# Offsets split earlier, constants on GpSimd, and three smaller moves in a fused GroupNorm, gating and deformable-convolution kernel

## The reference, cut to what matters

```python
def _L0(pair, Wa, ba, Wb, bb, Wg, bg, Wo, bo):     # gated products of the rows
    a = pair @ Wa + ba
    b = pair @ Wb + bb
    g = sigmoid(pair @ Wg + bg)
    ab = einsum('bijk,bikl->bijl', a, b)
    return g * ab @ Wo + bo

def _L1(x, w_off, b_off, w_def):                   # deformable 3x3 convolution
    x = relu(x)
    offset = conv3x3(x, w_off) + b_off             # 18 channels: dy, dx for 9 taps
    py, px = base_y + offset[:, :, 0], base_x + offset[:, :, 1]
    samp = bilinear_gather(x, py, px)              # 9 samples per pixel
    return einsum('bckhw,ock->bohw', samp, w_def)

x = x + _L0(group_norm(x), ...)
x = x + _L1(group_norm(x), ...)
```

## Time and profile before

| what | value |
|---|---|
| runs | 1631.22, 1642.09, 1646.17 us |
| profiled execution | 1645.54 us, span 1643.7 us, 28193 instructions |
| PE busy | 1543.9 us, 94% of the span |
| DVE busy | 1111.5 us, 68% |
| ACT busy | 1052.1 us, 64% |
| POOL busy | 934.0 us, 57% |
| granted clock of PE, mean | 0.986 of full speed |
| DMA | 356.56 MB, mean 217 GB/s |
| chain that ended last | PE 61%, issue 12%, POOL 8%, DVE 8%, DMA 6%, ACT 2% |

### The profile page before, as it was taken

How to read it: one execution, slowest core, us unless ns; L and a number is a source line. 1 busy time by engine, 2 the same in 40 slices (tenths; PEclk the granted TensorE clock), 3 DMA queues, 4 the chain that set the end, 5 groups by cost and what they waited for, 6 DMA issues and landing times.

```text
span 1643.7 us, 28193 instructions
## 1 busy us (share of the span) xinstructions
PE 1543.9 (94%) x9875; PEld 1129.6 (69%) x9876; DVE 1111.5 (68%) x1910; ACT 1052.1 (64%) x1500; POOL 934.0 (57%) x734
## 2 busy tenths in 40 slices
PE   4999999937999999999999999999999999999997
PEld 3777787715776667776666676766777677767775
DVE  5988888745666666666666666666666666666653
ACT  2555555527676767767667666666777777666662
POOL 2555555716755555655665656566566566656562
PEclk9999999958999999999999999999999999999999
DMA  4343344246767777777776777777767777777672
GB/s 138 107 119 106 118 118 118 75 166 241 262 260 247 253 240 268 252 253 246 247 251 243 242 252 255 246 249 272 261 237 256 254 256 268 261 243 247 242 238 67
DMA packets 145701, 356.56 MB, mean 217 GB/s; under 512 B 10709, under 2 KB 77808, under 8 KB 145584
## 3 DMA queue, kind: packets, MB, share of 16 engines
q1 hardware_dynamic: 130864, 327.90, 59.1%
q10 hardware_dynamic: 14720, 27.14, 4.7%
HBM read 292.14 MB, written 62.85 MB: 216 GB/s over the span
## 4 chain that ended last, share of the span: by engine, by line
PE 61%; issue 12%; POOL 8%; DVE 8%; DMA 6%; ACT 2%; SPq 0%; ACTq 0%; POOLq 0%; DVEq 0%
PE bank L759 24%; PE pair L731 17%; PE pair L805 7%; DMA hx_all<-hat_x 6%; POOL samples_hi L1496 4%; PE bank L777 4%; DVE offs_lo L1276 3%; PE pair L777 3%; POOL weights L1541 2%; DVE offs_hi L1273 2%; PE pair L742 2%; PE pair L744 2%; ACT samples_hi L985 1%; POOL rstd L1470 1%; POOL samples_lo L1483 1%
## 5 line engine op out<-in xcount | busy, mean ns | idle before, releaser
L1541 POOL TENSOR_TENSOR weights<-hy_all,hx_all 126x512 f32<-126x512 f32 x576 | 756.6, 1343 | 522.0 <-DMA hx_all<-hat_x 381.6
L1300 DVE SCALAR_TENSOR_TENSOR samples_lo<-bank,samples_hi 128x432 f16<-128x432 f32 (+1 forms) x704 | 403.4, 591 | 364.7 <-ACT samples_hi L985 351.5
L759 PE MATMUL bank<-weights,zT 126*128 126x216 f32 (+1 forms) x2816 | 583.0, 344 | 2.7 <-POOL weights L1541 2.3
L759 PEld LDWEIGHTS bank<-weights,zT 126*128 126x128 f32 x2816 | 490.2, 190 | 44.0 <-issue 29.2
L985 ACT ACTIVATE samples_hi<-bank 128x432 f16<-128x432 f32 (+1 forms) x704 | 362.4, 519 | 226.3 <-PE bank L759 216.2
L731 PE MATMUL pair<-samples_hi,w_hi 128*128 128x512 f16 x576 | 218.9, 380 | 1.2 <-DVE y L1334 1.2
L731 PE MATMUL pair<-samples_lo,w_hi 128*128 128x512 f16 x576 | 217.7, 378 | 0.0
L731 PE MATMUL pair<-samples_hi,w_lo 128*128 128x512 f16 x576 | 217.6, 378 | 0.0
L994 ACT COPY zT<-pair 126x512 f32<-126x512 f32 x192 | 112.5, 586 | 112.2 <-PE pair L777 108.0
L927 ACT ACTIVATE z<-raw,norm_band 128x2772 f32<-128x2772 f32 (+3 forms) x80 | 180.0, 2270 | 0.0
L1483 POOL TENSOR_TENSOR samples_lo<-samples_hi,samples_lo 128x512 f16<-128x512 f32 x64 | 74.2, 1159 | 131.1 <-ACT samples_lo L888 131.0
(11 more groups left out here) (138 smaller groups left out, 1944.8 us busy)
## 6 DMA issues: line engine op xcount, KB each, us to landing
hy_all<-hat_y SPq DMA_DIRECT2D x192, 648.0 KB
hx_all<-hat_x SPq DMA_DIRECT2D x192, 648.0 KB
raw<-x_pad SPq DMA_DIRECT2D x68, 272.0 KB, 11.2
x_pad<-hy_all SPq DMA_DIRECT2D x64, 272.0 KB, 3.3
weights<-in_x SPq DMA_DIRECT2D x64, 256.0 KB, 2.9
out<-y SPq DMA_DIRECT2D x32, 512.0 KB, 10.6
hat_y<-hats ACTq DMA_DIRECT2D x64, 252.0 KB
hat_x<-hats ACTq DMA_DIRECT2D x64, 162.0 KB
```

Source lines behind the costliest of these rows:

```text
L759: mm = nc.tensor.matmul(sampled_pair(b)[:, :, at:at + BR * cols], zT[0:WPIX, w, :], weights[0:WPIX, u, :, w * WC * BR:(w * WC + cols) * BR ...
L1300: nc.vector.scalar_tensor_tensor(out=samples_lo[:, u, :, c0:c1], in0=sampled_pair(b)[:, :, 0:c1 - c0], scalar=1.0, in1=samples_hi[:, u, :, ...
L1541: nc.gpsimd.tensor_tensor(weights[0:WPIX, u, k, :], hy_all[0:WPIX, k, :], hx_all[0:WPIX, k, :], ALU.mult).then_inc(weights_ready, 1)
```

## The change

The change does four things.

1. In `ORDER` the step P0 (the split of the offsets) moves from behind s6 to behind s5. Only DVE has a P step, so only DVE's list changes: there, P0 now precedes T1 and the low part of pair 6.
2. The memsets that DVE did between `norm_bias(0, 0)` and `scale_abg` are issued on POOL at the very start of its list. They signal a new semaphore `cleared`, which reaches 3, and SP and DVE wait for that instead of `const_set` at 7. The two memsets of `parts` become one.
3. The first two steps of `scale_abg` become a function of their own, `largest_abg`, called between `variance(0, 0)` and `norm_bias(0, 0)`.
4. ACT begins with a sigmoid of one column of constants.

```diff
@@ ORDER
-            "h0 s0 s1 s2 k0 h1 c0 c1 T0 k1 s3 s4 z0 z1 O0 k2 s5 c2 c3 T1 k3 s6 P0 s7 c4 T2 k4 c5 s8 Q0 "
+            "h0 s0 s1 s2 k0 h1 c0 c1 T0 k1 s3 s4 z0 z1 O0 k2 s5 P0 c2 c3 T1 k3 s6 s7 c4 T2 k4 c5 s8 Q0 "
@@ SP
-            sp.wait_ge(const_set, 7)
+            sp.wait_ge(cleared, 3)
@@ ACT
+            act.wait_ge(const_set, 3)
+            nc.scalar.activation(sigmoid_of[:], minus_half[:, 0:1], ACT.Sigmoid)
             act.wait_ge(in_f32, 160)
@@ DVE
-            def scale_abg():
+            def largest_abg():
                 dve.wait_ge(in_f32, 160)
                 nc.vector.scalar_tensor_tensor(out=w_abg_work[:], in0=w_abg[:], scalar=-1.0,
                 ...
                 nc.vector.tensor_reduce(abg_most[:], w_abg_work[:], AX.X,
                                         ALU.max).then_inc(abg, 1)
+
+            def scale_abg():
+
                 dve.wait_ge(abg, 3)
                 ...
                     variance(0, 0)
+                    largest_abg()
                     norm_bias(0, 0)
-                    nc.vector.memset(x1g, BELOW_ALL).then_inc(const_set, 1)
-                    nc.vector.memset(woff[:], 0.0)
-                    nc.vector.memset(bias_off[:], 0.0)
-                    nc.vector.memset(chosen, 0.0).then_inc(select_set, 1)
-                    nc.vector.memset(ramps[:], 0.0).then_inc(select_set, 1)
-                    nc.vector.memset(farthest[:], 0.0)
-                    nc.vector.memset(minus_one[:], -1.0).then_inc(const_set, 1)
-                    nc.vector.memset(parts[0:64, :], 0.0).then_inc(const_set, 1)
-                    nc.vector.memset(parts[64:128, :], 0.0).then_inc(const_set, 1)
-                    nc.vector.memset(pad_rows, BELOW_ALL).then_inc(pad_set, 1)
                     ...
-                    dve.wait_ge(const_set, 7)
+                    dve.wait_ge(cleared, 3)
                     scale_abg()
@@ POOL
+            nc.gpsimd.memset(minus_one[:], -1.0).then_inc(cleared, 1)
+            nc.gpsimd.memset(bias_off[:], 0.0)
+            nc.gpsimd.memset(parts[:], 0.0).then_inc(cleared, 1)
+            nc.gpsimd.memset(chosen, 0.0).then_inc(select_set, 1)
+            nc.gpsimd.memset(ramps[:], 0.0).then_inc(select_set, 1)
+            nc.gpsimd.memset(pad_rows, BELOW_ALL).then_inc(pad_set, 1)
+            nc.gpsimd.memset(farthest[:], 0.0)
+            nc.gpsimd.memset(woff[:], 0.0)
+            nc.gpsimd.memset(x1g, BELOW_ALL).then_inc(cleared, 1)
             pool.wait_ge(const_set, 3)
             ...
             pool.wait_ge(rows_copied, 1)
-            pool.wait_ge(const_set, 7)
```

More of the change, by code:

```diff
@@ L183, in preact_conv_kernel @@
         s6 = sb("s6", [P, BATCH, 6])
+        sigmoid_of = sb("sigmoid_of", [P, 1])
         mv1 = sb("mv1", [P, BR2, BATCH, 2])
@@ L249, in preact_conv_kernel @@
         const_set = sem("const_set")
+        cleared = sem("cleared")
         in_select = sem("in_select")
```

## The result

Over 22 runs each, the changed kernel took 1627.07 us in the median (1608.97 to 1648.15) and the kernel before 1645.2 (1631.22 to 1659.23). The ratio is 0.9881, with a 95% interval of 0.9854 to 0.9909. (The ratios here leave out runs over 1.5% above the fastest of their kernel; the medians hold all.) So it is faster by 1.2%, where the forecast of 1615 stood for 1.8% of the same median. The sign was right, the gain about two thirds of the forecast, and the median lies at the upper edge of the range, 0.07 us above its 1627. It also lies above the 1625.7 that the prediction, from its median of three runs, had set for "faster", and the interval reaches both sides of 0.99. The profiled execution, however, took 1617.48 us, 28 us less than that of before, and came within 3 us of the forecast. That is the first thing to be explained: the profiled execution is the second fastest of 22.

The account below looks back on a forecast made before the run. PE was taken to bound the bands; from the profiled 1645.5 us, 7.0 at the start and 26.2 in the bands gave a floor of 1612.3, plus 3 taken back: 1615. Forecast range 1608 to 1621; 8 in 10, 1609 to 1627.

Parts of the forecast that it names:

- The bound and the floor: Bands: PE bounds them, 19.22 us per quiet iteration; all gains taken from the profiled 1645.5 leave 1612.3 us.
- The start, -7.0 us: Before the bands: gate weights' maxima and split earlier, 6.0 us; ACT's second table load gone, 1.0 us.
- The constants on POOL: Start: POOL's memsets take 3.1 to 9.4 us, over before its first root at 10.36; cost 0, at worst +1.
- the table load: Start, ACT: one load can serve all, saving 1.0 us; by the skill's 2.66 us, up to 1.4 more.
- The split ends in time, -26.2 us: Bands, DVE: with P0 behind pair 5 the offsets' split ends before PE's Q0 needs it; all 26.2 us go.
- the work displaced behind the split: Bands, DVE: T1's copy and low parts of pairs 6 to 8 come later but in time; cost 0.
- What takes a part back, 3 us (0 to 6): Bands: the loop of hx loads and POOL's weights makes PE wait, costing 3 us over 59 bands.
- sign of being wrong: Bands: more than 10 us of PE's waits at line 759 for weights would show the take-over by the hats' DMAs.
- The first rival: Bands: the hats' DMAs take over in part at 19.42 us a round, 12 us come back: 1624; chance 0.20.
- Counting from the profiled execution: Whole kernel: terms subtracted from the profiled 1645.5 us, 3.4 over the median, as the floor is the same each run.
- The shared ports: Bands: DVE and POOL lock a port pair; moving the split exchanges collisions, so it takes 3.18 us at most.
- The other rivals: Bands: only the start pays, 1638.5 us, chance 0.09; or slower, the loop being the real pace, 1673, chance 0.04.

Follow-up runs that it names:

- e3_light: Changed kernel with hy_all loaded for the first band only, halving the bytes of the hats' loads: 1607.1 us, ratio 0.9742 to the kernel before.
- e4_before_light: Kernel before with hy_all loaded for the first band only, halving the bytes of the hats' loads: 1617.33 us, ratio 0.9866.
- e6_before_sixth: Kernel before with one hats' load in six left out (hy_all of the first group of taps, after the first band): 1618.84 us, ratio 0.9825.
- c1_after: Changed kernel run again without edit, against the kernel before: 1637.33 us in the median, ratio 0.9883.
- c2_after: Changed kernel run again without edit, on another chip, against the kernel before: 1632.17 us in the median, ratio 0.9900.
- e1_order: Kernel before with only P0 moved in ORDER, the start as before: 1652.0 us in the median, ratio 0.9958.
- Experiments 3 and 4: Hats' loads halved, then one load in six left out, each in both kernels: changed kernel 1607.1 and 1608.86 us, kernel before 1617.33 and 1618.84 us.
- e2_start: Changed kernel with the old ORDER, so only the start is changed: 1646.34 us in the median, ratio 0.9899.
- v3_ahead4: Changed kernel with AHEAD 4 instead of 3 and four hat buffers, so hats run a band further ahead: 1707.5 us, ratio 1.0248.

## Why the prediction was right, and where it was too large

- **The bound and the floor.** Right. PE bounds the bands, the quiet iteration is 19.22 us, and five kernels show it. The floor was put at 1612.3; e3_light has 1607.1. Beside the trace of before, the 5 us that are missing are in two stretches taken as 0: up to the fifth Q0 e3_light is 9.4 us ahead (406.8 against 416.2) where the start's term was 7.0, and behind the last Q0 it needs 64.9 us instead of 67.3.
- **The start, -7.0 us.** Right: 5.93 us at PE's first group (17.64 instead of 23.57) and 7.16 at the second. The split's last subtraction gained 0.93, and DVE's scaling lost about as much (14.90, 1.11 us), beside POOL's subtraction that now ran with it. The constants on POOL were written in 4.15 us (0.70 to 4.85), near the lower end of 3.1 to 9.4. The second group gained 1.23 us more than the first, about PE's wait of 1.09 for the sigmoid behind the load. On the table load the row decides against the 2.66 us of the Trainium skill (ScalarE: Activation LUTs, the section What ACT_TABLE_LOAD costs): the load took 1.28, the activation behind it started at 29.81, and no drain shows.
- **The split ends in time, -26.2 us.** The mechanism is right: there is no wait of PE before Q0 after 400 us in any profiled execution with P0 in the new place, and the work displaced behind the split cost next to nothing: after 400 us PE waits 0.6, 0.7 and 0.9 us for samples_lo in the three executions of the changed kernel, and never for zT. The reading of its cause was half right. It named POOL's multiplications beside the split, but not why they stood there in some iterations and not in others; e4_before_light and e6_before_sixth show that it is the late loads.
- **What takes a part back, 3 us (0 to 6).** This is the term that was mis-sized. It measured 4.2 us in the execution profiled first, but in c1_after, c2_after and e1_order PE's waits for weights were 17.4, 16.2 and 24.3 us, over the 10 us that the prediction had named as its sign of being wrong, and with the slower clock behind the longer ones the excess was 25.8, 26.8 and 39.0. In medians the changed kernel gained 18.1 us (1645.2 - 1627.07). Of these, 10.2 are the start and the first iterations (1617.33 - 1607.1), so of the bands' 26 us about 8 were kept. This puts times of different batches together. The same sum on the chip of c1_after leaves 2.6 us (1650.17 - 1637.33 - 10.2), on that of c2_after 12.0 (1654.19 - 1632.17 - 10.0). So the share kept varies widely, and the near hit of the first profiled execution was in part luck.
- **Why it was mis-sized.** The excess of 26.2 us was read as DVE's, and the weights' 0.4 us as the loop's. But late loads show at two places. PE waited at the first, before Q0, and while it did the loop caught up, so little was left for the second. Experiments 3 and 4 show that both waits have this one cause; that the first made room for the second is only a reading. Against it stands e2_start, which kept the first wait (15.8 us) and had 12.5 us of the second beside it: in a slow execution the first wait doesn't prevent the second. The first rival, in which the hats' DMAs take over in part, was the better number for the typical execution with its 1624; it had 0.20.
- **Counting from the profiled execution** was sound for the floor, but for the 5 us above, and misleading for the remainder, which varies with the loads between executions, by 39 us in the changed kernel.
- **The shared ports.** The Trainium skill (SBUF — State Buffer, the section Who interferes with whom) was used to say that moving the split exchanges its collisions. The traces agree where they can: offs_lo is short in all bands of e4_before_light, where POOL has ended. In the first profiled execution of the changed kernel its median is above the 1.16 us of the earlier trace rows, with a longest of 1.73 over the bound of 1.645 that was assumed; in c1_after, where the loads are later, the median is 0.69.

  Line 1274 of the changed kernel, in the columns of the earlier trace rows:

```profile
L1274 DVE TENSOR_TENSOR offs_lo<-offs,offs_hi x64: 691/1637/1725, 344.1 to 1544.2; 114x512 f16<-114x512 f32 x64
```

- **The other rivals** fell: the start was not all, and nothing became slower.

## What to carry to other kernels

Where a wait is removed that is long in some iterations and absent in others, ask what differs between them before its whole sum is booked as gain. If the cause is something late that also feeds a second wait further on, the first wait may have been giving it time, and a part of it, perhaps all, comes back at the second; here, 26 us were expected of the bands and 3 to 12 were kept. Leaving out a part of the suspected transfers, with every instruction of the engines kept, shows in one run whether two waits have one cause. And one profiled execution tells the floor well and the remainder badly.

## What the runs showed of the hardware that was not expected

- The duration of the loads' packets differs between executions of one kernel: 117, 122 and 125 ns over all of q1, with spans of 1615.7, 1640.6 and 1641.0 us. With a sixth fewer bytes the runs of the changed kernel lay within 6 us, where c2_after on the same chip had 24.
- A wait of PE of 3.04 us cost 4.8 in c1_after: the granted clock was 0.50 for about 3 us behind it. A wait of 3.05 us in v3_ahead4 (up to 1028.96) cost 3.3, with the granted clock at 1.00 throughout, and one of 1.64 us in the changed kernel cost 1.9.
- With the hats a band earlier (v3_ahead4) the DMA engines moved less in the same time, 232 instead of 260 GB/s, and a packet took 133 ns instead of 117.
